# Cross-attention: the softmax sums by TensorE with ones instead of GpSimd, batches without a loop, the shift's rows by a whole-array transpose

## The reference

```
def _L0_xattn_ref(q, k, v, Wq, bq, Wk, bk, Wv, bv, Wo, bo):
    qh = proj(q, Wq, bq)
    kh = proj(k, Wk, bk)
    vh = proj(v, Wv, bv)
    scores = jnp.einsum('bhqd,bhkd->bhqk', qh, kh) / math.sqrt(D_K)
    attn = jax.nn.softmax(scores, axis=-1)
    out = jnp.einsum('bhqk,bhkd->bhqd', attn, vh)
    concat = out.transpose(0, 2, 1, 3).reshape(B, -1, D_MODEL)
    return concat @ Wo.T + bo
...
x = x + _L0_xattn_ref(_layernorm(x, axis=-1), ctx_1024, ctx_1024, ...)
x = x + _L0_ffn_ref(_layernorm(x, axis=-1), L0_ffn_w_gate, L0_ffn_w_up, L0_ffn_w_down)
```

## Time and profile before

| | us |
|---|---|
| median of 3 runs (lowest, highest) | 2568.3 (2564.93, 2572.62) |
| the profiled execution: time | 2569.35 |
| the profiled execution: its span | 2567.3 |
| start and weights, to the first score of batch 0 | 62.8 |
| batch 0 | 91.0 |
| batches 1 to 14 | about 1535 |
| batch 15 and the end of the attention | about 111 |
| weights' transposes and the feed-forward part | about 767 |

### The profile page before, as it was taken

How to read it: one execution, slowest core, us unless ns; L and a number is a source line. 1 busy time by engine, 2 the same in 40 slices (tenths; PEclk the granted TensorE clock), 3 DMA queues, 4 the chain that set the end, 5 groups by cost and what they waited for, 6 DMA issues and landing times. The chain is left out here.

```text
span 2567.3 us, 46677 instructions
## 1 busy us (share of the span) xinstructions
PE 2236.7 (87%) x15012; PEld 1846.1 (72%) x15012; DVE 2028.4 (79%) x3101; ACT 850.8 (33%) x1677; POOL 785.2 (31%) x484
## 2 busy tenths in 40 slices
PE   4989888798888889888898878887499999999998
PEld 4777667676667667676676667674378888888887
DVE  4878778787877678777787877776689999999986
ACT  3434344343434334343343434333311111111111
POOL 0444444444434434443434434445000000000000
PEclk9989899898989889988998989897799999999999
DMA  4342333433233342333433233332500101101000
GB/s 149 96 118 76 108 84 109 115 78 110 75 108 95 93 111 78 101 86 104 116 77 110 73 106 84 103 85 56 163 22 29 37 25 37 33 28 37 25 25 25
DMA packets 136288, 204.70 MB, mean 80 GB/s; under 512 B 33872, under 2 KB 84560, under 8 KB 133568
## 3 DMA queue, kind: packets, MB, share of 16 engines
q1 hardware_dynamic: 136128, 202.22, 28.1%
HBM read 75.67 MB, written 23.33 MB: 39 GB/s over the span
## 5 line engine op out<-in xcount | busy, mean ns | idle before, releaser
L617 DVE TENSOR_REDUCE row_max<-max_bank 112x1 f32<-112x376 f32 (+1 forms) x1024 | 524.3, 540 | 343.8 <-PE max_bank L475 338.9
L722 POOL TENSOR_TENSOR prob_sum<-prob_sum,probs 125x896 f32<-125x896 f32 x256 | 556.1, 2172 | 491.0 <-ACT probs L542 479.7
L542 ACT ACTIVATE probs<-score_bank 125x448 f32<-125x448 f32 x768 | 405.7, 543 | 379.4 <-PE score_bank L490 374.7
L475 PE MATMUL max_bank<-k_high,q_masked 128*112 128x376 f32 (+1 forms) x1024 | 349.6, 385 | 143.1 <-DVE row_max L617 71.8
L490 PE MATMUL score_bank<-qstack,kstack 100*128 100x224 f32 x1536 | 319.5, 295 | 69.7 <-issue 66.1
L490 PEld LDWEIGHTS score_bank<-qstack,kstack 100*128 100x128 f32 x1536 | 279.8, 203 | 116.7 <-issue 104.0
L475 PEld LDWEIGHTS max_bank<-k_high,q_masked 128*112 128x112 f32 x1024 | 176.5, 190 | 227.7 <-DVE row_max L617 105.0
L717 POOL TENSOR_TENSOR prob_sum<-probs 125x896 f32<-125x896 f32 x64 | 138.6, 2166 | 379.5 <-ACT probs L542 294.8
L449 PE MATMUL proj_bank<-wv_hi,ctx_hi 128*128 128x256 f32 x768 | 226.2, 294 | 4.3 <-DVE wo_lo L696 4.3
L1115 PE MATMUL gate_bank<-ffn_gate_hi,f_xqt 128*128 128x512 f32 (+1 forms) x672 | 218.8, 387 | 8.1 <-DVE f_xqt L1221 8.1
L505 PE MATMUL pv_bank<-probs,values 125*32 125x224 f32 x3072 | 221.7, 411 | 0.0
(11 more groups left out here) (120 smaller groups left out, 4523.8 us busy)
## 6 DMA issues: line engine op xcount, KB each, us to landing
kstack<-k_high SPq DMA_DIRECT2D x512, 93.8 KB, 2.2
ctx_raw<-in_ctx SPq DMA_DIRECT2D x16, 1500.0 KB, 7.0
kstack<-k_low SPq DMA_DIRECT2D x256, 93.8 KB, 2.2
qstack<-q_part SPq DMA_DIRECT2D x768, 28.0 KB, 1.8
ffn_quant<-fw_share SPq DMA_DIRECT2D x48, 176.0 KB, 1.8
fw_raw<-ffn_quant SPq DMA_DIRECT2D x33, 256.0 KB, 4.1
xn<-in_x SPq DMA_DIRECT2D x16, 448.0 KB, 8.4
q_masked<-q_part SPq DMA_DIRECT2D x256, 28.0 KB, 1.8
```

Source lines behind the costliest of these rows:

```text
L475: nc.tensor.matmul(out[0:QH, 0:hi - lo], q_masked[t % 2][:, j, half * QH:(half + 1) * QH], k_part[t % 2][0][:, lo:hi], start=True, stop=Tr ...
L542: nc.scalar.activation(probs[p][:, j, :, :], score_bank[j % 2][0:KW, 0:2 * SQ].rearrange("p (k q) -> p k q", k=2), ACT.Exp, scale=float(DK ...
L617: nc.vector.tensor_reduce(row_max[:, half, j, kh:kh + 1], mbank[0:QH, 0:KSPLIT[kh + 1] - KSPLIT[kh]], AX.X, ALU.max).then_inc(max_reduced, 1)
L722: nc.gpsimd.tensor_tensor(prob_sum[:, :, :], prob_sum[:, :, :], probs[p][:, :, k, :], ALU.add).then_inc(summed, 1)
```

## The change

1. The POOL additions into `prob_sum` go, with the tile, its semaphores and ACT's and DVE's waits for them. Each `pv` unit gets 8 more matmuls on PE, ones by the same probabilities, into the second half of `pv_bank` and accumulated over the 6 key tiles. The `sum` unit goes. DVE's `inverse` waits for the third `pv` unit.
2. `phases` has no loop: all 16 batches are written out.
3. `neg_max` has 128 columns, zero except for 96 to 100, and `shift` is a transpose into all 128 partitions of the bank.

```diff
-    add(at["sum"], ("sum", g - 1))
...
-    neg_max = sb("neg_max", [QH, 2, HG])
+    neg_max = sb("neg_max", [QH, 2, P])
...
-        with engine.Fori(1, batches - 1) as b:
-            body(b, batch_units(False, False), list(v_end), list(m_end))
+        for b in range(batches - 1):
+            body(b, batch_units(b == 0, False), list(v_end), list(m_end))
...
-                    nc.tensor.matmul(out[SHIFT:STK, 0:QH], neg_max[:, u[2], :], ident[0:QH, 0:QH],
-                                     start=True, stop=True).then_inc(made["shift"], 1)
+                    nc.tensor.transpose(out[:, 0:QH], neg_max[:, u[2], :],
+                                        ident[0:QH, 0:QH]).then_inc(made["shift"], 1)
...
-                                                    probs[p][:, j, k, :], start=(kt == 0), stop=(kt == KT - 1))
+                                                    probs[p][:, j, k, :], start=(kt == 0), stop=(kt == KT - 1),
+                                                    skip_group_check=True)
+
+                        for j in range(HG):
+                            last = nc.tensor.matmul(pv_bank[t % 2][j * DK:(j + 1) * DK, SQ:2 * SQ], ones[0:KW, :],
+                                                    probs[p][:, j, k, :], start=False, stop=(kt == KT - 1),
+                                                    skip_group_check=True)
                     last.then_inc(made["pv"], 1)
-                elif kind == "sum":
-                    reached(pe, summed, 5 * (b * NG + t) + 5)
-                    for j in range(HG):
-                        last = nc.tensor.matmul(pv_bank[t % 2][j * DK:(j + 1) * DK, SQ:2 * SQ], ones[0:KW, :],
-                                                prob_sum[:, j, :], start=True, stop=True)
-                    last.then_inc(made["sum"], 1)
...
-                        reached(act, summed, 5 * (b * NG + t - 1) + 2 * p + 1)
...
-                    dve.wait_ge(made["sum"], count(b, "sum", t))
+                    reached(dve, made["pv"], count(b, "pv", t, 2))
...
-                if kind == "pv":
-
-                    p = u[2]
-                    base = 5 * (b * NG + t)
-                    pool.wait_ge(exp_done, count(b, "score", t, p, HG - 1))
```

More of the change, by code:

```diff
@@ L251, in start_units @@
     return units + v[4:5] + m[15:16] + v[5:6] + [("shift", 0, 1)]
-END_UNITS = [("pv", 3, 2), ("sum", 3), ("inverse", 3, 0), ("inverse", 3, 1), ("heads", 3), ("heads_hi", 3), ("sum_lo", 3), ("out", 0, 0), ("out", 0, 1)]
+END_UNITS = [("pv", 3, 2), ("inverse", 3, 0), ("inverse", 3, 1), ("heads", 3), ("heads_hi", 3), ("sum_lo", 3), ("out", 0, 0), ("out", 0, 1)]
 def attention(nc, ctx, dram, ident, ln_consts, x1, ffn_raw, ffn_quant, batches):
@@ L294, in attention @@
              for idle, n in ((in_values, 0), (in_probs, 0), (in_probs, 1), (in_values, 0))]
-    prob_sum = sb("prob_sum", [KW, HG, SQ])
     heads = sb("heads", [P, SQ])
@@ L314, in attention @@
     pv_bank = [bank(f"pv_bank{i}") for i in range(2)]
-    names = ("score", "max", "shift", "k", "q", "v", "xt", "out", "pv", "sum")
+    names = ("score", "max", "shift", "k", "q", "v", "xt", "out", "pv")
     made = {n: sem(f"{n}_made") for n in names}
@@ L327, in attention @@
     normalized = sem("heads_normalized")
-    summed = sem("probs_summed")
     stats_done = sem("ln_stats")
@@ L340, in attention @@
     low_stacked = sem("low_stacked")
+    neg_zeroed = sem("neg_max_zeroed")
     mask_zeroed = sem("q_mask_zeroed")
@@ L393, in phases @@
         m_end = [("max", 0, 15), ("shift", 0, 1)]
-        body(0, batch_units(True, False), list(v_end), list(m_end))
-        with engine.Fori(1, batches - 1) as b:
-            body(b, batch_units(False, False), list(v_end), list(m_end))
+        for b in range(batches - 1):
+            body(b, batch_units(b == 0, False), list(v_end), list(m_end))
         v_last = [("v", 0, 1, KT - 2), ("v", 0, 1, KT - 1)]
@@ L621, in body @@
                         reached(dve, made["shift"], count(b, "shift", t - 1, half))
-                        nc.vector.tensor_reduce(neg_max[:, half, :], row_max[:, half, :, :], AX.X, ALU.max,
+                        nc.vector.tensor_reduce(neg_max[:, half, SHIFT:STK], row_max[:, half, :, :], AX.X, ALU.max,
                                                 negate=True).then_inc(max_negated, 1)
@@ L697, in body @@
                                             w_hi_lo[t][0][:, :, :].bitcast(F32), ALU.subtract).then_inc(w_lo_done, 1)
+        nc.vector.memset(neg_max[:, :, :], 0.0).then_inc(neg_zeroed, 1)
         nc.vector.memset(ones[:, :], 1.0).then_inc(consts_made, 1)
@@ L702, in _ @@
         dve.wait_ge(small_loaded, 64)
+        dve.wait_ge(neg_zeroed, 1)
         phases(dve, body)
@@ L709, in body @@
                 kind, t = u[0], u[1]
-                if kind == "pv":
-                    p = u[2]
-                    base = 5 * (b * NG + t)
-                    pool.wait_ge(exp_done, count(b, "score", t, p, HG - 1))
-                    if p == 0:
-                        reached(pool, made["sum"], count(b, "sum", t - 1))
-                        nc.gpsimd.tensor_tensor(prob_sum[:, :, :], probs[0][:, :, 0, :], probs[0][:, :, 1, :],
-                                                ALU.add).then_inc(summed, 1)
-                    else:
-                        for k in range(2):
-                            pool.wait_ge(summed, base + 2 * p - 1 + k)
-                            nc.gpsimd.tensor_tensor(prob_sum[:, :, :], prob_sum[:, :, :], probs[p][:, :, k, :],
-                                                    ALU.add).then_inc(summed, 1)
-                elif kind == "norm":
+                if kind == "norm":
                     n = 2 * (b + t) + u[2]
```

## The result

| | us | ratio to before, 95% interval |
|---|---|---|
| before, beside it | 2566.6 | |
| changed kernel | 2435.1 (2433.1 to 2439.2) | 0.950 (0.945 to 0.956) |
| its profiled execution, span | 2433.8 | |

The kernel is 131 us faster; 70 were forecast, with at most 112 in the range. Span against span it is 133.5: batches 1 to 14 give 114.6 (66 were forecast), batch 15 with the end of the attention 16.9 (8), batch 0 gives 3.0 (4 lost were forecast), the start costs 1.0, and the feed-forward part is unchanged.

A forecast was written before the change was run, and what follows sets the result against it. PE does most work, but DVE's end and SP's chain set slot 0. Terms of -4.7 us a batch times 14 (-66), batch 0 +4 and batch 15 -8 gave -70 on 2569.35: 2499 us, range 2456 to 2545.

The forecast's parts named there:

- the largest term: Slot 0 with its wait: DVE ends earlier, so SP's chain starts earlier, -3.8 us a batch.
- `stack_low` starts 7.0 - 3.8 = 3.2 us behind PE's end.: End of slot 3: L868 and L869 fall to 0.53, L866 keeps 2.72, SP loses its branch; start moves from 7.0 to 3.2.
- Slots 1 and 3: +1.4 each, less 0.8.: PE's added work costs 1.4 us in each slot; shorter waits for DVE give back 0.8 in both together.
- Slot 2: -2.9.: Wait for DVE's row maximum -2.6 us, low clock behind it -1.7, PE's added work +1.4.
- The loop gone: 0.: Start of slot 0: removing the 5.27 us issue stall brings 0 a batch, being covered by SP's chain.
- 14 x 5.3 = 74 us: What the skill's instruction-fetch rule, read alone, would promise for the loop's stall; the prediction did not count it.
- PE has about 27 us in slot 0.: PE's own time up to the `q_masked` wait, added work included: about 27 us or less, against 30.3 for SP's chain.
- The cover: Slot 0: PE's added work hides under SP's chain; without it 1.4 us in each of 14 batches, 20 us.
- more: Rival: chain to the first maximum only 25.4 us, shifts, sums and low clock slightly better, -3.1 a batch: 2456 us, 16%.
- the anchor of slot 0 itself: Slot 0 with its wait, 7.0 + 27.1 = 34.1 us, set by DVE's end and SP's chain, not by PE.

The follow-up runs named there:

- e3: Changed kernel with the shift made by the earlier 4-column matmul in the strip at 96: 2455.6 us, ratio 0.962.
- e1: Kernel before with only its loop over the batches written out: 2515.9 us, ratio 0.985.
- e2: Changed kernel with the loop put back: 2419.6 us, ratio 0.948.
- e4: Changed kernel plus 5 POOL multiplications per group on a private tile nobody reads, where the additions had been: 2465.8 us, ratio 0.965.
- e14: Changed kernel with the loop put back, run again in more rounds on the changed kernel's chip: 2425.5 us, ratio 0.946.

## Why the prediction was right in direction and too small

The mechanisms held: POOL's work holds DVE, DVE's end holds SP, SP's chain with `q_masked` ends last in slot 0 before and after, and the loop's stall was worth little there. What failed were sizes, nearly all in the same direction, and first of all the largest term, the start of SP's chain: -3.8 us a batch in the sum, -6.1 measured.

- **"`stack_low` starts 7.0 - 3.8 = 3.2 us behind PE's end."** It was 0.7. The step let only L868 and L869 shrink and kept L866 at the 2.72 of batch 5. But L866 fell to 0.34 as well, in all 14 batches. The 2.72 was no property of that step: in the kernel before it took 2.7 in 3 of the 14 batches, 2.2 in 5 and 0.33 in 6, and other steps were held in its place. In the changed kernel L866's successor starts 1.8 us ahead of PE's end (1.2 at best before) and the bias additions start 0.9 ahead (1.6 before), so they come when it is past. -2.5 a batch. The chain behind it grew by 0.8, where 0 was forecast; whether by other traffic or by SP's own queue was not separated. Net -1.4 a batch, some 20 us.
- **"Slots 1 and 3: +1.4 each, less 0.8."** +0.4 in both together. In slot 3 of batch 5 the account is: three `pv` units +2.3 as forecast; the `sum` unit -0.70, its neighbours being shorter without it by 0.2 in all (0.5 forecast, 0.38 by streaming alone; the row was nearer, and still short); two shifts -0.55 with theirs (0.4 forecast; e3 has 0.5); a wait for DVE -0.66. 1.6 a batch, 23 us.
- **"Slot 2: -2.9."** -3.3 on average. The wait of 3.13 went and the low clock behind it too (1.00 now, 0.53 in a part before), as forecast. Before, slot 2 had 27.8 us in some batches and 26.4 in others, and only a 26.4 had been read. 6 us.
- **"The loop gone: 0."** In the changed kernel straight-line code costs about 11 us instead. In the kernel before it gave 37, with bias additions that start later and with little from the stall. The stall is there at 13 passages, so the 14 x 5.3 = 74 us of the prediction counts one too many.
- **"PE has about 27 us in slot 0."** It has 21.0 in batch 5. The 27 was made from the 29.6 of batch 1, of which only the wait of 5.03 was taken down, to 1.5. In that stretch another 1.3 us were a wait for `neg_max`, and the 4 us behind the long wait ran at a granted clock of 0.50; all of this is gone. The cover was 6 us thicker than thought, which changed no term in batches 1 to 14; the wait for `q_masked` became 7.2 us on average where 3 to 5 were forecast. In batch 15, where no `q_masked` chain covers PE, slot 0 alone gave 6 of the 17 us (8 were forecast). Batch 0 gained 3.0 instead of losing 4; its granted clock is 1.00 instead of 0.96, and the rest was not taken apart. 16 us for both.

Together 65 us, where the span fell by 63 more than forecast. That the direction and the main mechanisms came true is no luck, but the size rested on one batch. The range was too narrow for the same reason: the rival "more" let the terms shrink by 0.1 us each and not the anchor of slot 0 itself, on which the largest term rested. Its price had been read at one place of one batch, while the 14 batches of the same trace already showed the held step changing.

## What to carry to other kernels

When an engine in the middle of a chain is slow because another blocks it, don't price the instructions that stand beside the blocker in one batch. Read the same place in all batches: if the held instruction changes from one to the next, it is a race, and a shift of one microsecond can decide whether it costs 4 us or nothing, as in e1. Before paying for a stall, ask which wait ends last behind it; the one of 5.1 us a batch here could be taken away for next to no gain, while the place of four small DMAs in the queues was worth some 120 us. And here a load of 1.5 MB issued just ahead of four small DMAs that the next step needed cost some 90 us.

## What the runs showed of the hardware

- A loop's branch on PE took 3.3 to 3.9 us (up to 4.5 in e2) or 0.2, by where the code lies: 80 waits ahead of the loop decided it. In one layout another 3.1 to 3.7 us followed with all semaphores reached.
- A DVE operation on 128x352 elements that takes 0.53 us took 1.5 to 2.9 beside POOL's additions or multiplications, of a tile of its own (e4) or not, and 4.92 where it met several in a row.
- PE ran at 0.50 of its clock behind a wait of 7.47 us and at 1.00 behind one of 1.15 (e14).
- 4 DMAs of 28 KB landed 7.8 us after their issue behind a load of 1.5 MB, and 2.6 ahead of it.
- A transpose of the whole array took 0.03 to 0.25 us up to the next instruction where a 4-column matmul in a strip took 0.28.
- GpSimd issued 4 DMAs in 2.1 us, about as fast as SP (2.4).
